# Eight-head attention row sums moved from VectorE passes into ScalarE's exponentials, with every engine's step list laid anew

## The reference

```python
h = relu(layernorm(x)); x = x + L0(h)   # four-head GAT, elu, one-head GAT, elu, FFN, layernorm
h = relu(layernorm(x)); x = x + L1(h)   # eight-head attention, masked by adj
h = relu(layernorm(x)); x = x + L2(h)   # deg*(h Wi + b) + adj (h Wj)
h = relu(layernorm(x)); x = x + L3(h)   # one-head GAT
# L1, per graph and head (d = 32):
scores = (q @ k.T) * scale              # 128x128
attn = softmax(where(adj == 0, -inf, scores), axis=-1)
out = (attn @ v) merged over heads @ Wo.T + bo
```

## Time and profile before

| what | value |
|---|---|
| median of 3 executions | 2682.75 us (2681.85 to 2684.97) |
| the profiled execution's own time | 2683.62 us |
| its span, first to last instruction | 2681.8 us |
| TensorE matmul (PE) busy | 2580.8 us, 96% of the span |
| VectorE (DVE) busy | 2304.7 us, 86% |
| ScalarE (ACT) busy | 2061.2 us, 77% |
| GpSimd (POOL) busy | 1248.4 us, 47% |
| DMA | 44.29 MB moved, mean 17 GB/s |

### The profile page before, as it was taken

One profiled execution on the slowest core, in us unless ns is written; L12 is line 12 of the kernel. 1 busy time (PEld: TensorE's weight loads), 2 busy tenths in 40 slices (PEclk: granted clock), 3 DMA queues, 4 the chain that ended last, 5 costly groups with the idle time before them and its releaser, 6 DMA issues.

```text
span 2681.8 us, 64380 instructions
## 1 busy us (share of the span) xinstructions
PE 2580.8 (96%) x21761; PEld 2333.0 (87%) x21761; DVE 2304.7 (86%) x8352; ACT 2061.2 (77%) x5708; POOL 1248.4 (47%) x2015
## 2 busy tenths in 40 slices
PE   4899999999999999999999999999999999999985
PEld 3789999998998998999999999899999899999874
DVE  5689889889888888888888888888988988988884
ACT  4688788787787887877877877878878878878752
POOL 3545445444444444454454454454544544544431
PEclk9999999999999999999999999999999999999986
DMA  4000000000000000000000000000000000000000
GB/s 131 1 2 9 17 17 9 17 17 14 13 17 13 13 17 17 10 17 17 10 17 17 10 17 17 10 17 17 9 17 17 9 17 17 10 17 13 9 9 12
DMA packets 41286, 44.29 MB, mean 17 GB/s; under 512 B 2816, under 2 KB 40448, under 8 KB 40832
## 3 DMA queue, kind: packets, MB, share of 16 engines
q1 hardware_dynamic: 40816, 39.14, 4.6%
q10 hardware_dynamic: 144, 1.05, 0.1%
HBM read 23.40 MB, written 16.78 MB: 15 GB/s over the span
## 4 chain that ended last, share of the span: by engine, by line
PE 70%; ACT 20%; POOL 4%; issue 3%; DVE 2%; SPq 1%; DMA 0%; ACTq 0%; DVEq 0%; POOLq 0%
PE pA L1084 12%; PE pB L1191 11%; PE pE L1084 7%; PE pB L1158 7%; PE pB L1084 7%; ACT probs L579 7%; PE pF L1315 4%; PE pC L1084 3%; ACT pA L573 3%; ACT B_h_high L613 2%; PE pF L1328 2%; PE pA L1302 2%; PE pC L1237 2%; ACT C_hid_t L649 2%; ACT whs L560 1%
## 5 line engine op out<-in xcount | busy, mean ns | idle before, releaser
L677 ACT ACTIVATE F_s_t<-F_s_t,F_m 128x128 f32<-128x128 f32 x1024 | 325.3, 395 | 0.9 <-DVE F_m L863 0.8
L1191 PE MATMUL pB<-wout_high,B_h_high 128*128 128x258 f32 x1024 | 307.4, 300 | 1.1 <-DVE B_h_low L897 1.1
L1191 PE MATMUL pB<-wout_low,B_h_high 128*128 128x258 f32 x1024 | 289.6, 283 | 0.0
L1191 PE MATMUL pB<-wout_high,B_h_low 128*128 128x258 f32 x1024 | 288.8, 282 | 0.0
L1158 PE MATMUL pB<-probs,whs 128*128 128x128 f32 x2048 | 285.4, 282 | 1.4 <-ACT wh L620 1.1
L1158 PEld LDWEIGHTS pB<-probs,whs 128*128 128x128 f32 x2048 | 254.2, 192 | 20.8 <-issue 2.4
L1084 PE MATMUL pA<-wh_high,A_hT_high 128*128 128x512 f32 x512 | 229.0, 447 | 9.5 <-POOL wh_low L388 8.4
L889 DVE SCALAR_TENSOR_TENSOR B_e<-B_e,pB 128x512 f32<-128x512 f32 x256 | 172.9, 675 | 71.7 <-ACT B_e L605 71.4
L464 POOL TENSOR_TENSOR B_h_low<-B_e,B_h_high 128x512 fp32r<-128x512 f32 x128 | 165.8, 1295 | 111.8 <-ACT B_h_high L613 111.8
L1084 PE MATMUL pA<-wh_high,A_hT_low 128*128 128x512 f32 x512 | 202.9, 396 | 0.0
L1084 PE MATMUL pA<-wh_low,A_hT_high 128*128 128x512 f32 x512 | 202.7, 396 | 0.0
(11 more groups left out here) (261 smaller groups left out, 10046.6 us busy)
## 6 DMA issues: line engine op xcount, KB each, us to landing
xs<-in_x SPq DMA_DIRECT2D x64, 256.0 KB, 2.7
out_x<-xs SPq DMA_DIRECT2D x64, 256.0 KB, 2.1
probs<-in_a_heads ACTq DMA_DIRECT2D x1, 1024.0 KB, 4.9
F_pT<-in_w_heads SPq DMA_DIRECT2D x2, 512.0 KB, 6.9
xs<-in_w_out SPq DMA_DIRECT2D x1, 1024.0 KB, 9.6
F_s_t<-in_wijT SPq DMA_DIRECT2D x1, 512.0 KB, 6.4
C_h_t<-in_a_out SPq DMA_DIRECT2D x1, 256.0 KB, 9.9
D_q_t<-in_w SPq DMA_DIRECT2D x1, 256.0 KB, 7.2
```

What stands on the lines that cost most here:

```text
L677: last = act.activation(F_s_t[:, s, h, :], F_s_t[:, s, h, :], ACT.Exp, scale=-1.0, bias=F_m[:, s, h:h + 1])
L1191: last = pe.matmul(pB[:, 0, 0:D + 2], a, w[:, k, :], start=(k == 0 and i == 0), stop=(k == KH - 1 and i == 2))
```

## The change

`F_sum_step` is gone from VectorE. Each of the sixteen exponentials of `F_exp` per pair writes its row sum through ScalarE's accumulator into `F_sum` instead, waits first for the previous pair's `F_recip`, and `F_recip` now waits for the exponentials. A wait in `x_there` on an earlier `A_moments` is dropped. All four lists are laid anew.

```diff
-A_fleft:3 A_fright:3 A_rstd:2 E_right:9 E_rstd3:8 C_hb:5 C_low:5 B_lowh.1:4 D_xb:6 E_fcopy:8 E_rstd:7 C_xb:2 C_fcopy:4
-C_rstd:5 E_xb:7 D_rstd:5 B_lowh.0:3
+E_rstd:7 A_rstd:1 E_xb:7 D_rstd:5 A_fleft:2 B_lowh.0:3 A_fright:2 C_hb:4 D_xb:5 C_xb:2 E_rstd3:7 C_low:4 E_fcopy:7
+B_lowh.1:3 E_right:7 C_rstd:4 C_fcopy:3
...
                     done(act, "F_max" + part, g)
-                    for h in range(c * HPC, (c + 1) * HPC):
-                        last = act.activation(F_s_t[:, s, h, :], F_s_t[:, s, h, :], ACT.Exp, scale=-1.0, bias=F_m[:, s, h:h + 1])
+                    before(act, "F_recip", p)
+                    for i in range(c * HPC, (c + 1) * HPC):
+                        h = F_heads[i]
+                        last = act.activation(F_s_t[:, s, i, :], F_s_t[:, s, i, :], ACT.Exp, scale=-1.0, bias=F_m[:, s, i:i + 1],
+                                              accum_out=F_sum[:, s, h:h + 1])
                     last.then_inc(S["F_exp" + part], 1)
...
             def x_there(g, p):
 
-                before(dve, "A_moments", g - 1)
                 dve.wait_ge(x_loaded, 16 * (p + 1))
...
-            def F_sum_step(part, c):
-
-                def step(g, p, s):
-                    done(dve, "F_exp" + part, g)
-                    pairs = slice(c * HPC // K, (c + 1) * HPC // K)
-                    total = F_sum[:, s, :].rearrange("p (c j) -> p j c", c=K)[:, pairs, :]
-                    e = F_s_t[:, s, :, :].rearrange("p (j c) m -> p j c m", c=K)[:, pairs, :, :]
-                    dve.tensor_reduce(total, e, AX.X, ALU.add).then_inc(S["F_sum" + part], 1)
-                return of_graph(step)
-
             def F_recip(p):
 
-                both(dve, "F_suma", p)
-                both(dve, "F_sumb", p)
+                both(dve, "F_expa", p)
+                both(dve, "F_expb", p)
                 dve.reciprocal(F_rec[:, :, :], F_sum[:, :, :]).then_inc(S["F_recip"], 1)
```

More of the change, by code:

```diff
@@ L24 @@
 PE_ORDER = """
[L25 to L28, removed]
+C_fT:3 A_f:1 E_pT:7 C_s:3 F_s:5 E_o:7 A_wh_lo.0:1 C_pT:3 B_oh.0:2 E_zT:6 A_wh_hi.0:1 A_wh_lo.1:1 E_m.0:6 C_o:3
@@ L29 @@
+F_pTb.0:5 F_pTa.0:5 B_wh0.0:2 B_wh1.0:2 B_wh2.0:2 E_m.1:6 B_wh3.0:2 D_zT:4 F_pTb.1:5 C_hT:3 F_pTa.1:5 E_am:6 B_ol.1:2
+D_k:4 C_hid:3 A_s.0:1 F_rT:5 F_o:5 D_v:4 E_zT3:6 A_wh_hi.1:1 B_oh.1:2 C_ffn:3 E_h:6 A_s.1:1 F_out:5 A_pT.0:1 E_fT:6
+B_wh0.1:2 B_wh1.1:2 A_zT:0 E_s:6 B_wh2.1:2 B_wh3.1:2 D_q:4 B_ol.0:1 A_pT.1:1
 """.split()
 ACT_ORDER = """
-A_whc_lo.0:1 B_highh.0:2 E_mjhigh.0:6 F_pTca.0:5 F_expb.1:5 F_pTcb.0:5 D_high:4 C_oexp.0:3 C_oexp.1:3 E_mjhigh.1:6
-B_whc.0:2 F_pTca.1:5 F_pTcb.1:5 D_kc:4 C_hhigh:3 A_whc_lo.1:1 B_negl.1:2 F_high:5 B_expl.1:2 C_hidc:3 A_leaky.0:1
@@ L33 @@
[L33 to L36, removed]
+A_whc_hi.0:1 C_hhigh:3 B_negl.1:2 F_pTcb.1:5 F_pTca.1:5 A_whc_lo.1:1 D_kc:4 B_expl.1:2 C_hidc:3 A_leaky.0:1 C_high:3
+E_hT3:6 B_highl.1:2 A_exp.0:1 F_high:5 B_negh.1:2 A_whc_hi.1:1 B_exph.1:2 E_hc:6 A_leaky.1:1 B_highh.1:2 A_attn.0:1
@@ L37 @@
+A_exp.1:1 E_leaky:6 B_whc.1:2 A_high:0 E_exp.0:6 E_exp.1:6 D_qc:4 B_negl.0:1 A_attn.1:1 E_attn:6 A_fround:0 C_leaky:2
+B_expl.0:1 C_exp.0:2 C_exp.1:2 F_expa.0:4 C_attn:2 A_whc_lo.0:0 B_negh.0:1 E_high:5 B_exph.0:1 B_highl.0:1 F_expb.0:4
+B_highh.0:1 F_expb.1:4 E_mjhigh.0:5 F_pTcb.0:4 C_oexp.0:2 C_oexp.1:2 F_expa.1:4 F_pTca.0:4 E_mjhigh.1:5 D_high:3
+B_whc.0:1
 """.split()
 DVE_ORDER = """
-F_maxb.0:5 C_max.0:3 A_frest:1 C_max.1:3 B_hl.0:2 E_low:6 C_x1.1:4 F_maxb.1:5 B_lowl.0:2 D_stats.0:4 D_moments.0:4
@@ L40 @@
[L40 to L44, removed]
@@ L45 @@
-C_stats.1:3 C_g.0:3 E_z.0:5 C_moments.1:3 E_max.0:6 E_max.1:6 C_g.1:3 A_low:0 F_maxa.0:4 F_maxa.1:4 C_fTc:2 E_recip:6
-E_z.1:5 E_left.0:6 E_left.1:6 C_x1.0:3
+B_lowl.1:4 B_hh.1:4 C_y:5 A_max.1:3 C_stats.0:5 C_stats.1:5 E_fTc:8 C_moments.0:5 F_x2:7 C_g.0:5 C_moments.1:5
+E_max.0:8 A_recip.1:3 E_max.1:8 E_stats.0:7 A_norm.1:3 E_stats.1:7 E_moments.0:7 E_moments.1:7 C_g.1:5 A_low:2
+C_x1.0:5 D_stats.0:5 A_moments.0:1 C_fTc:4 C_x1.1:5 E_z.0:7 E_z.1:7 A_moments.1:1 A_frest:2 D_moments.0:5 C_max.0:4
@@ L47 @@
+C_max.1:4 F_maxa.0:6 F_maxa.1:6 E_recip:8 E_left.0:8 E_left.1:8 F_maxb.0:6 B_hl.0:3 D_stats.1:5 E_low:7 D_moments.1:5
+B_hh.0:3 F_maxb.1:6 B_lowl.0:3 D_z.0:5 D_z.1:5 C_recip:4 E_mjlow.0:7 E_mi.0:7 C_min:4 A_z.0:1 C_h.0:4 F_recip:6
+C_h.1:4 A_z.1:1 A_stats.0:0 E_mjlow.1:7 E_mi.1:7 D_low:5 F_rb:6 C_hlow:4 E_x3:7 E_stats3.0:7 E_stats3.1:7 A_stats.1:0
+E_moments3.0:7 E_moments3.1:7 F_rTc:6 E_z3.0:7 E_z3.1:7 B_hl.1:3 A_max.0:2 F_on:6 D_vc:5 A_recip.0:2 F_low:6
+A_norm.0:2
 """.split()
 POOL_ORDER = """
-A_fleft:3 A_fright:3 A_rstd:2 E_right:9 E_rstd3:8 C_hb:5 C_low:5 B_lowh.1:4 D_xb:6 E_fcopy:8 E_rstd:7 C_xb:2 C_fcopy:4
@@ L59 @@
 D_stats D_moments D_rstd D_z D_xb D_zT D_high D_low D_k D_kc D_v D_vc D_q D_qc
-F_s F_maxa F_maxb F_expa F_expb F_pTa F_pTb F_pTca F_pTcb F_o F_suma F_sumb F_recip F_rb F_rT F_rTc F_on F_high F_low
+F_s F_maxa F_maxb F_expa F_expb F_pTa F_pTb F_pTca F_pTcb F_o F_recip F_rb F_rT F_rTc F_on F_high F_low
 F_out F_x2
@@ L1051, in _ @@
                 **pair("F_maxa", F_max("a", 0)), **pair("F_maxb", F_max("b", 1)),
-                **pair("F_suma", F_sum_step("a", 0)), **pair("F_sumb", F_sum_step("b", 1)),
                 "F_recip": F_recip, "F_rb": F_rb, "F_rTc": copy("F_rT", "F_rTc", F_rT_t[:, :], pF[:, 1, :]), "F_on": F_on,
```

## The result

The changed kernel takes 2671.37 us in the median (2669.87 to 2673.38), the kernel before on the same chip 2683.86 us: the ratio is 0.9955, with a 95% interval of 0.9943 to 0.9967. The time fell by 12.5 us where 20 were forecast. The profiled execution took 2670.69 us, its span is 2668.7.

What follows compares the result with a forecast made beforehand. TensorE's own work, busy 99.4% of the steady stretch, was taken to set the round. 60 x (-0.10 - 0.20) = -18, start -2, drain 0 gave -20 us: 2662.7 us in the median, range 2652 to 2687.

Steps and rivals of the forecast that it cites:

- Part 1: Row sums moved from VectorE to ScalarE: 2.6 us a round less on VectorE, 1.4 more on ScalarE, costed at 0.
- the last rival: Four reads per step cost ScalarE more than they save VectorE; alone 2682.75 us, chance within the first rival's 0.2.
- Part 2: VectorE's `A_frest`, too late for PE's `A_wh_lo.0`, should be on time by 0.3 us: -0.10 us a round.
- Part 3: PE's `E_fT` waits for GpSimd's split of `E_f`; two thirds of the 0.29 us excess goes: -0.20 us a round.
- the second rival: A VectorE chain through `C_max`, `F_maxa`, `E_left` delays `E_zT` and bounds the round; 0.5 us late gives 2693 us; chance 0.15.
- The steady sum: Gain of the full rounds from the two waits: 60 x (-0.10 - 0.20) = -18 us.
- two waits: PE's weight loads wait on `E_f` from GpSimd (0.29 us excess) and `A_f_t` from VectorE (0.10): 0.39 us a round.
- Part 4: At the start, `wh_low` ahead of `C_xb` lets `A_wh_lo.0` begin at about 25.6 instead of 28.3 us: -2 us.
- Part 5: In the drain, longer exponentials, sums gone behind them, same chain of the last pair's E steps: 0, bounds -4 and +5.

Runs made afterwards that it cites:

- lists_only: The changed kernel's lists with the row sums left in VectorE's four passes; 2674.41 us, 0.9969 of the kernel before.
- early_dots: early_max with only the weight dot products, `wh_low` and the masks moved at the start; 2644.54 us, 0.9859 of the kernel before.
- early_dots_passes: early_dots with the row sums in VectorE's four passes, at the places of lists_only; 2645.52 us, 0.9856 of the kernel before.
- acc_only: The kernel before with its lists kept and only the row sums moved into ScalarE's accumulators; 2726.25 us, 1.0163 of the kernel before.
- split_beside_sbuf: early_max with VectorE's SBUF-only `B_lowl.1` moved behind `B_hh.1`, beside GpSimd's split of `E_f`; 2651.16 us, 0.9883 of the kernel before.
- early_max: The changed kernel with ScalarE's `A_fround` moved ahead of `E_attn` and VectorE's `D_moments.0` ahead of `A_frest`; 2647.68 us, 0.9871 of the kernel before.

## Why the prediction was right, and where it was not

- **The sign and the range were right**, 2671.4 in 2652 to 2687, and so was the reading of the kernel before: PE sets the round, work taken from VectorE gives nothing (lists_only against the change, early_dots against early_dots_passes). In the changed kernel PE's work and one chain of VectorE set it together. The size was off by 8.7 us, and part of the gain came from terms that I had at nothing.
- **Part 1, the sums at 0**: right in the new lists, wrong as stated. "What hides it is the idle time of 6.5 us a round" is an average over ScalarE's round; acc_only had idle time left too and lost 43 us, since three `F_exp` steps stood ahead of a copy that PE needs. By the same error the last rival, "that alone gives 2682.75", is refuted. The reads' price (0.09 us each) and ScalarE's 83% came as forecast. VectorE came to 85%, not 82%: it lost 1.7 us a round and not 2.6, since some of its other operations take longer at their new places (the last section has one).
- **Part 2, `A_frest` -0.10**: the wait is gone. `A_frest` ended 1.54 us behind the last product of `A_f` (1203.69 to 1205.23) where 1.6 was worked out, and PE came to `A_wh_lo.0` 2.10 us behind it, where 1.9 was.
- **Part 3, `E_fT` -0.20**: the excess of 0.29 went whole. All four operations of the split take 0.20 us in the change. I had taken two thirds; the end that the Trainium skill gives in "SBUF — State Buffer", section "SBUF: two separate sides" (a VectorE operation with two SBUF inputs and a GpSimd operation that reads SBUF exclude each other), was the right one, and split_beside_sbuf shows its mechanism: one such neighbour makes one of the four 0.72 us long.
- **The step that failed is the second rival.** It saw the chain `C_max`, `F_maxa`, `E_left` on VectorE without a margin, but took `E_zT` as the one that waits, and counted `B_oh.0` as 0.9 us of PE work that covers the chain. `B_oh.0` itself writes the bank that `F_maxa` reads, so the chain must be over before it and not behind it. By the prediction's own units PE comes to `B_oh.0` 1.4 + 0.45 + 1.4 + 0.25 = 3.5 us after `A_f`, and VectorE ends `F_maxa` after 1.6 + 0.4 + 1.7 = 3.7, or 3.9 with `D_moments.0` (0.21), which stands in the list between `A_frest` and `C_max` and was left out: a wait of 0.4 us. `E_zT` has no wait for `E_left` in the steady stretch; `B_oh.0` waits in every round, 0.40 us, 63 x 0.40 = 25 us. The price of the mechanism (6 us for each 0.1) was right, its place was wrong, and it came together with the gain and not in its stead. That the total still fell into the range is partly luck: this loss of 25 us, which the sum did not have, stood against gains that it did not have either.
- **The steady sum**: two waits give 0.39, the new one takes 0.40, and the round still fell by 0.12. The round of early_max, with no wait left, is 39.957 - 39.434 = 0.52 us below before, so 0.13 us of PE's time before lay outside the two waits that I priced. The traces show where it is not: no third wait on another engine stands among the weight loads of the kernel before. Distances from product to product, as means over 40 rounds, show it spread: the eight products of a `B_oh` or `B_ol` step take 0.89 to 1.00 us to the start of the next step before and 0.81 to 0.89 in early_max, and other steps, with another step behind them than before, differ by some 0.1 us in both directions. So the 0.13 us may come from PE's order itself; that is argued from the traces, and no run isolates it.
- **Part 4, the start, -2**: measured -1.8, by another way. `A_frest` came at 26.75 and the first product at 27.24, not at 25.6. VectorE waited for the second pair's load until 14.04 us, close to the 14.4 worked out, but behind it one dot product was held for 2.1 us by `wh_low`, and this term was missing.
- **Part 5, the drain, 0**: measured -3.4, within its bounds. It was put at 0 because the chain of the last pair's steps is the same; the rows have the 3.4 us in PE's busy time and clock, and no run shows what caused them.
- So the rounds gave 7.9 us for a forecast of 18, the start 1.8 for 2, the drain 3.4 for 0.

## What to carry to other kernels

For a wait that a new order may create, list every reader of every bank that the next PE step writes: a consumer's end matters to whoever reuses its bank, not only to the step that takes its result. An engine's idle share does not say that an addition is free; the steps behind it and their waiters do, so 1.4 us of reads a round cost 43 us here in one place and nothing a few entries further. And take a mixed change apart in both directions: here the headline edit was worth nothing that could be measured, the lists gave the gain, and two more entries moved in them gave twice as much again.
